# Row-sum reciprocals of a whole attention head spread by DMA, the head normalised in one operation, and one output copy per block

## The chip, the cores and the metric

The kernel runs on one core of one Trainium2 chip. The metric is the device time of one execution in microseconds (us), the median of several runs. A profile of one execution shows every instruction of the five engines: TensorE (PE, with its weight loads as PEld), VectorE (DVE), ScalarE (ACT), GpSimd (POOL) and SyncE (SP, which here only issues DMAs).

## The reference

One block of a metaformer on x of 8 images, 512 channels and 1024 positions, all in fp32: a channel layernorm, attention with 8 heads of 64 channels over the 1024 positions, a residual, a layernorm over channels, and a mixture of 16 experts that each choose their 128 best rows of every image.

```python
x = x + conv_ref(ln_c(x), Wq, bq, Wk, bk, Wv, bv, Wo, bo)
    # q, k, v = projections; scores = q k^T / 8 for each head
    # attn = softmax(scores); out = attn v; then the projection with Wo
t = to_tokens(x)
t = t + ffn_ref(ln_t(t), gate_weight, w1, b1, w2, b2)
    # logits = t gate; affinity = softmax(logits)
    # for each expert the top 128 rows: gelu(x w1 + b1) w2 + b2, times the gate, added back
x = from_tokens(t, x)
```

## The kernel before

`attention` runs first, over the 8 images one after the other; `experts` follows. Nothing of the two overlaps. Each engine has its own program, written out by hand in the order in which it issues; semaphores tie them together, so the order of the code is the schedule. To get fp32 precision from the fast matmul format every operand is split into a high part (written by ScalarE, `..._hi`) and a low part (the rest, `..._lo`), and products are the sum of high and low terms.

In an image, heads are taken in pairs. A pair has 16 units of 128 queries (8 for each head); the 64 units of an image are walked by a step number `s`. TensorE makes the scores of unit `s` (L834), VectorE their negated row maxima (L669), ScalarE the exponentials with their row sums `rsum` (L466). Two steps later TensorE turns the probabilities (L845) into the two-deep buffer `ring`, ScalarE writes the high part of `PT` (L475) and VectorE the low part (L727). Two units make a block `m` of 256 queries, 32 blocks in an image, 4 in a head. TensorE multiplies a block with `V` into the PSUM tile `O` (L877); half of the sum lies on the 64 partitions of the head and half on the other 64.

The normalisation of a block takes the rest of the engines. VectorE writes the reciprocals of its two columns of row sums (`rinv`, L735). GpSimd spreads each column over 128 columns (`rinv_bc`, L395, two instructions a block). TensorE turns both into the right half of `O` (`inverse_sums`, L889), so that the reciprocals lie along the columns. ScalarE copies three parts of 64 partitions out of PSUM (`copy_output`, L523 to L525: `Rs`, `oH`, `oL`). GpSimd adds the two halves (L410) and multiplies with the reciprocals (L413) into `oT`. From there `high_of_output` (ScalarE, L515) and `low_of_output` (GpSimd, L378) split the pieces of `oT` for the projection with Wo (`project_out`, L914). The pieces of the first three pairs are split while the last head still runs, at the steps of `EARLY_AT` and the blocks of `EARLY_BLOCK`.

The residual rows of x are loaded by SyncE late in the image, into `oT` and `spare`, as soon as the pieces that lay there are split. GpSimd adds the bias of the projection to them (`add_bo`, L384): tiles 0 to 3 beside the last two blocks, tiles 4 to 7 after the last piece. VectorE adds the projection to each tile (`tile_t`), takes its statistics, and between those normalises the next image's tiles `xt` (`normalise`, L630), in the order of the list `WRAP`. TensorE turns those tiles for the next image (L801) and projects V.

At the end of a pair TensorE projects q and k of the next pair (`project_pair`), and SyncE copies halves of k to the other partitions (`duplicate_k`) and loads the pair's weights (`load_pair`).

In `experts` the tiles are allocated one after the other; `b1s`, `idxc` and `gatec` have 32, 64 and 64 bytes to a partition and stand ahead of the larger tiles.

Of the kernel before, what the change touches and what calls it, by code (L numbers as in the profile page):

```python
# [16 lines left out]
F32 = mybir.dt.float32  # L17
F32R = mybir.dt.float32r
U32 = mybir.dt.uint32
# [58 lines left out]

def attention(nc, x, wT, b_row, b_col, gate, out, n2_dram, aff_dram, ident):
# [6 lines left out]
    wqk_dram, wv_dram = split_weights_dram(nc)  # L86
    with ExitStack() as ctx:
# [27 lines left out]
        def res(i):  # L115
# [5 lines left out]
        tmp = sb("tmp", [P, 3, 2, QC])  # L121
        Rs = tmp[:, 0, :, :]
        oL = tmp[:, 1, :, :]
        oH = tmp[:, 2, :, :]
        n2T = tmp[:, 0:2, :, :].rearrange("p a q c -> p a (q c)").rearrange(
            "p a (k t) -> p a k t", k=KC)
# [7 lines left out]
        ones = sb("ones", [P, P])  # L134
        rinv_bc = sb("rinv_bc", [P, 2, 2, P])
# [33 lines left out]
        res_in = [sem(f"res_in{i}") for i in range(2)]  # L169
# [27 lines left out]
        rbc_done = sem("rbc_done")  # L197
        pv_read = sem("pv_read")
        pv_done = sem("pv_done")
        o_copied = sem("o_copied")  # L200
        o_sum = sem("o_sum")
# [38 lines left out]
        def blocks_of_piece(j):  # L240

            if j < EARLY:
                return j // 2 * NT + QB + 2 * (j % 2) + 2
            return BLOCKS - QB + (j - EARLY) + 1
# [19 lines left out]
        def _(sp):  # L264
# [51 lines left out]
            def image(b, last):  # L316
# [11 lines left out]
                for k in range(2):  # L328
                    sp.wait_ge(os_lo, b * PIECES + 2 * k + 2)
                    sp.dma_start(dst[:, k, :, :], src[:, 2 * k:2 * k + 2, :]).then_inc(res_in[0], 16)  # L330
                sp.wait_ge(os_lo, b * PIECES + EARLY)
                sp.dma_start(dst[:, 2, :, :], src[:, 4:6, :]).then_inc(res_in[1], 16)
                sp.dma_start(spare[:, :, :], src[:, 6:8, :]).then_inc(res_in[1], 16)
# [26 lines left out]
        def _(pool):  # L360
# [8 lines left out]
            pool.wait_ge(ones_set, 1)  # L369
# [3 lines left out]
            def image(b, last):  # L373
                def low_of_output(j, blocks):
                    chunk, cols = piece(j)
                    pool.wait_ge(o_norm, b * BLOCKS + blocks)
                    pool.wait_ge(os_hi, b * PIECES + j + 1)
                    nc.gpsimd.tensor_tensor(oS[:, 1, chunk, cols], oT[:, chunk, cols],  # L378
                                            oS[:, 0, chunk, cols].bitcast(F32), ALU.subtract).then_inc(os_lo, 1)

                def add_bo(i):
                    if i % 4 == 0:
                        pool.wait_ge(res_in[i // 4], b * 32 + 32)
                    nc.gpsimd.tensor_tensor(res(i), res(i), bo_bc[:, :], ALU.add).then_inc(xbo, 1)  # L384

                for k in range(BLOCKS + 2):
                    if k < BLOCKS:
                        if k >= 3:
                            pool.wait_ge(o_norm, b * BLOCKS + k - 2)
                        pool.wait_ge(rinv_done, b * BLOCKS + k + 1)  # L390
                        if k >= 2:
                            pool.wait_ge(pv_done, b * BLOCKS + k - 1)
                        pool.sem_inc(pool_passed, 1)
# [4 lines left out]
                    if k >= 2:  # L398
                        m = k - 2
                        pair, odd, q = m // NT, m // QB % 2, m % QB  # L400
                        rows = slice(D * odd, D * odd + D)

                        if k < BLOCKS:
                            pool.wait_ge(rbc_done, b * BLOCKS + k + 1)
                        elif k == BLOCKS:
                            pool.wait_ge(xbo, b * NT + 4)
                        else:
                            pool.wait_ge(os_lo, b * PIECES + PIECES - 1)
                        pool.wait_ge(o_copied, b * BLOCKS + m + 1)
                        nc.gpsimd.tensor_tensor(oH[rows, m % 2, :], oH[rows, m % 2, :], oL[rows, m % 2, :],  # L410
                                                ALU.add).then_inc(o_sum, 1)
# [3 lines left out]
                        for j in range(EARLY):  # L415
                            if EARLY_BLOCK[j] == k:
                                low_of_output(j, m + 1)
                        if m >= BLOCKS - QB:
# [983 lines left out]
```

## Time and profile before

| | |
|---|---|
| time, median of 3 runs | 3360.12 us (3359.72 to 3362.19) |
| the profiled execution | 3358.84 us, its span in the trace 3357.0 us |
| TensorE busy | 3154.9 us, 94% of the span |
| VectorE busy | 2319.4 us, 69% |
| ScalarE busy | 2003.8 us, 60% |
| GpSimd busy | 1294.3 us, 39% |
| last image's attention ends | about 2485 us; the experts take the rest |

The busy share of an engine is an average over stages with different limits; ends of matmuls are modelled, so TensorE's pace is read from the distance between starts. In a timeline several like instructions that follow each other are merged into one row with their count; a bracket gives the idle time of the engine before the row and what ended it.

### The profile page before, as it was taken

Reading aid. Unit: us, or ns where it says so; the run is one execution under the profiler, and the core shown is the slowest. Engines: PE = TensorE matmul, PEld = TensorE weight load, DVE = VectorE, ACT = ScalarE, POOL = GpSimd, SP = SyncE. Lnnn points to the kernel's source line nnn. Section 1 sums busy time; section 2 is a strip of 40 time slices with the busy share of each in tenths; the row PEclk is TensorE's granted clock in tenths of the full one; section 3 lists DMA queues with packets and bytes.
Section 4 is the critical chain, followed back from the end, with each engine's and each line's share of the span. In section 5 each row is a group of like instructions: output and inputs, shape, how many; then the busy total and the mean of one; then the engine's idle time right before and its main releaser. Section 6 shows DMA issues by size and latency. Waiting matters only on the chain. (4 is left out here: it accounts for less than half of the span.)

```text
span 3357.0 us, 51875 instructions
## 1 busy us (share of the span) xinstructions
PE 3154.9 (94%) x18562; PEld 2696.9 (80%) x18562; DVE 2319.4 (69%) x3649; ACT 2003.8 (60%) x3833; POOL 1294.3 (39%) x1536
## 2 busy tenths in 40 slices
PE   6999999999999999999999999999944999999998
PEld 5888888788878888887888888888833888888886
DVE  5877687678768776875877677667766556555553
ACT  4876678478748856883887578478821333333332
POOL 1335234423523352343335234523432444444443
PEclk9999999999999999999999999999977999999999
DMA  6012111310220131112103211310132565655654
GB/s 219 26 51 101 52 51 39 113 52 26 82 96 26 51 109 51 44 51 101 52 27 101 77 41 40 111 39 26 39 114 61 135 133 126 142 136 120 149 136 59
DMA packets 108907, 268.82 MB, mean 80 GB/s; under 512 B 13456, under 2 KB 21648, under 8 KB 97936
## 3 DMA queue, kind: packets, MB, share of 16 engines
q1 hardware_dynamic: 80016, 198.80, 17.6%
q0 software_dynamic: 28672, 67.13, 11.2%
q8 instruction: 134, 2.20, 0.3%
q14 instruction: 85, 0.70, 0.1%
HBM read 158.40 MB, written 73.92 MB: 69 GB/s over the span
## 5 line engine op out<-in xcount | busy, mean ns | idle before, releaser
L727 DVE TENSOR_TENSOR PT<-ring,PT 128x512 fp32r<-128x512 f32 x1024 | 675.7, 685 | 230.8 <-ACT PT L475 221.8
L877 PE MATMUL O<-PT,V 128*128 128x256 f32 x4096 | 677.0, 290 | 0.0
L669 DVE TENSOR_REDUCE nmax<-S 128x1 f32<-128x1024 f32 x512 | 619.4, 1210 | 78.1 <-PE S L834 78.0
L395 POOL TENSOR_SCALAR rinv_bc<-ones,rinv 128x128 f32<-128x128 f32 x512 | 303.6, 605 | 934.3 <-DVE rinv L735 931.5
L845 PE MATMUL ring<-ident,prob 128*128 128x128 f32 x4096 | 617.2, 274 | 38.6 <-DVE qs L662 19.4
L475 ACT ACTIVATE PT<-ring 128x512 fp32r<-128x512 f32 x1024 | 582.1, 598 | 84.9 <-PE ring L845 70.5
L877 PEld LDWEIGHTS O<-PT,V 128*128 128x128 f32 x4096 | 577.7, 189 | 39.1
L466 ACT ACTIVATE prob<-S,nmax 128x1024 f32<-128x1024 f32 x512 | 571.7, 1117 | 56.3 <-DVE nmax L669 56.3
L834 PE MATMUL S<-kd,qs 128*128 128x512 f32 x2048 | 594.7, 414 | 3.4 <-DVE qs L662 2.3
L845 PEld LDWEIGHTS ring<-ident,prob 128*128 128x128 f32 x4096 | 460.3, 140 | 83.8 <-issue 70.4
L834 PEld LDWEIGHTS S<-kd,qs 128*128 128x128 f32 x2048 | 349.1, 189 | 55.5 <-ACT prob L466 2.8
L1356 PE MATMUL p<-ws,hT 128*128 128x512 f32 x1536 | 381.6, 400 | 0.0
L1319 PE MATMUL p<-xT,ws 128*128 128x512 f32 x1536 | 366.2, 397 | 1.5 <-DVE xT L1247 1.5
L1319 PEld LDWEIGHTS p<-xT,ws 128*128 128x128 f32 x1536 | 290.2, 189 | 72.3 <-issue 1.9
L1356 PEld LDWEIGHTS p<-ws,hT 128*128 128x128 f32 x1536 | 281.5, 188 | 61.9 <-DVE hT L1262 0.3
L1156 POOL DMA_INDIRECT out_dram<-y,idxc x128 | 203.2, 1588 | 291.7 <-ACT y L1224 264.3
L410 POOL TENSOR_TENSOR tmp<-tmp 64x256 f32<-64x256 f32 x256 | 189.1, 739 | 312.0 <-ACT tmp L525 292.5
L789 PE MATMUL ring<-nT,wqk 128*128 128x512 f32 x1152 | 267.3, 391 | 3.7 <-DVE PT L727 2.9
L789 PEld LDWEIGHTS ring<-nT,wqk 128*128 128x128 f32 x1152 | 214.4, 188 | 51.3 <-issue 7.9
L1212 ACT ACTIVATE hf<-p,b1s 128x512 f32<-128x512 f32 x128 | 88.2, 689 | 244.1 <-PE p L1319 244.1
L914 PE MATMUL S<-wo,nT 128*128 128x512 f32 x768 | 204.0, 418 | 0.0
L1199 ACT ACTIVATE xT<-xr 128x512 fp32r<-128x512 f32 x128 | 72.9, 598 | 207.9 <-PE xr L1329 207.9
(115 smaller groups left out, 3840.7 us busy)
## 6 DMA issues: line engine op xcount, KB each, us to landing
kd<-kd SPq DMA_DIRECT2D x128, 256.0 KB, 3.7
wraw<-w_dram SPq DMA_DIRECT2D x32, 1024.0 KB, 6.7
wqk<-wqk_split SPq DMA_DIRECT2D x24, 1024.0 KB, 4.8
xt<-x_dram SPq DMA_DIRECT2D x16, 1024.0 KB, 7.5
PT<-wv_split SPq DMA_DIRECT2D x7, 2048.0 KB, 8.2
oT<-x_dram SPq DMA_DIRECT2D x24, 512.0 KB, 3.6
out_dram<-oT SPq DMA_DIRECT2D x48, 256.0 KB, 8.3
n_rows<-oT SPq DMA_DIRECT2D x48, 256.0 KB, 2.3
```

The costliest lines, as they stand in the source:

```text
L395: last_bc = nc.gpsimd.tensor_scalar(rinv_bc[:, k % 2, j, :], ones[:, :], rinv[:, 2 * k + j:2 * k + j + 1], None, ALU.mult)
L466: nc.scalar.activation(prob[:, s % 2, :], S[:, s % 2, :], ACT.Exp, bias=nmax[:, s:s + 1], accum_out=rsum[:, s:s + 1]).then_inc(exp_done, 1)
L475: nc.scalar.activation(PT[:, 0, u // 2 % 2, 4 * c:4 * c + 4, u % 2 * P:u % 2 * P + P], ring[:, k % 2, :].rearrange("p (m q) -> p m q", m=4 ...
L669: nc.vector.tensor_reduce(nmax[:, s:s + 1], S[:, s % 2, :], AX.X, ALU.max, negate=True).then_inc(max_done, 1)
L727: nc.vector.tensor_tensor(PT[:, 1, here[0], here[1], here[2]], ring[:, k % 2, :].rearrange("p (m q) -> p m q", m=4), PT[:, 0, here[0], her ...
L789: last_mm = nc.tensor.matmul(dst, l, r, start=(n == 0), stop=(n == len(pairs) - 1))
L834: last_mm = nc.tensor.matmul(S[:, s % 2, 512 * m:512 * m + 512], qs[:, odd, i * P:(i + 1) * P], kd[:, odd, l, 512 * m:512 * m + 512], star ...
L845: last_t = nc.tensor.transpose(ring[:, k % 2, m * P:(m + 1) * P], prob[:, u % 2, (4 * c + m) * P:(4 * c + m + 1) * P], ident)
L877: last_mm = nc.tensor.matmul(O[:, m % 2, 0:QC], V[:, t, head // 2, 2 * (head % 2):2 * (head % 2) + 2, :].rearrange("p h d -> p (h d)"), PT ...
L914: last_mm = nc.tensor.matmul(S4[:, i % 4, :], oS[:, l, c, i * P:(i + 1) * P], wo[:, w, c, :], start=(c + n == 0), stop=(c == KC - 1 and n ...
L1319: last = nc.tensor.matmul(dst, l, r, start=(n == 0), stop=(n == len(pairs) - 1))
L1356: prod = nc.tensor.matmul(p2[:, j, :], hT[:, l, c, j * P:(j + 1) * P], ws[:, k, w, KC + c, :], start=(c + n == 0), stop=(c == KC - 1 and n ...
```

## The change

The reciprocals of heads 0 to 6 no longer go through GpSimd and TensorE. VectorE makes them once for a head (8 columns). SyncE writes them to a row of 1024 in DRAM and reads that row back to the 64 partitions of the head in the new tile `Rs` (`spread_inverse`, two DMAs and three waits in SyncE's program). GpSimd multiplies a whole head of `oT` with `Rs`, after its fourth block, in one instruction over 64 partitions and 1024 columns; it reads `Rs` with a step of 8 elements. The last head keeps the way through TensorE, block by block, but TensorE reads the column of `rinv` directly, with a step of 0, in place of the copy that GpSimd made.

`copy_output` is one copy of 128 partitions and 256 columns to `oHL`; for the last head a second one brings the reciprocals. GpSimd then moves the other half to the head's partitions (a copy, `oS2`) and adds both halves straight into `oT`. The wait of the copy for the block two before is now on this sum (`o_sum`) and no longer on the normalised block.

The residual loads and `add_bo` move: tiles 6 and 7 are loaded at the start of the image and added at block 5; tiles 0 to 5 are added at blocks 26 to 29 (`RES_TILES`), each ahead of that block's sum. In `experts`, the four small tiles are allocated last.

```diff
+RES_TILES = {5: [6, 7], 26: [0, 1], 27: [2], 28: [3, 4], 29: [5]}
+HEAD_UNITS = NT
+HEAD_BLOCKS = NT // 2
+NORMS = H - 1 + HEAD_BLOCKS
...
+    rinv_rows = nc.dram_tensor("rinv_rows", [H - 1, N], F32).ap()
...
-        tmp = sb("tmp", [P, 3, 2, QC])
...
+        Rs = sb("Rs", [P, N])
+        oHL = sb("oHL", [P, 2, QC])
+        oS2 = sb("oS2", [P, 2, QC])
...
-                for p in range(1, PAIRS):
-                    duplicate_k(b, p)
-                    if p < PAIRS - 1 or not last:
-                        sp.wait_ge(ring_filled, b * RING + ring_proj(p, 3) + 1)
-                        load_pair(p % (PAIRS - 1) + 1)
...
+                def spread_inverse(h):
+                    row, units = rinv_rows[h:h + 1, :], slice(HEAD_UNITS * h, HEAD_UNITS * h + HEAD_UNITS)
+                    odd = h % 2
+                    sp.wait_ge(rinv_done, b * NORMS + h + 1)
+                    sp.dma_start(row.rearrange("a (p u) -> p (a u)", p=P), rinv[:, units]).then_inc(rinv_out, 16)
+                    sp.wait_ge(rinv_out, b * (16 * (H - 1)) + 16 * h + 16)
+                    if h >= 2:
+                        sp.wait_ge(o_norm, b * NORMS + h - 1)
+                    sp.dma_start(Rs[D * odd:D * odd + D, :], row.broadcast_to([D, N])).then_inc(Rs_in[odd], 16)
+
+                load_residual(3)
+                for h in range(H - 1):
+                    if h % 2 == 1:
+                        p = h // 2 + 1
+                        duplicate_k(b, p)
+                        if p < PAIRS - 1 or not last:
+                            sp.wait_ge(ring_filled, b * RING + ring_proj(p, 3) + 1)
+                            load_pair(p % (PAIRS - 1) + 1)
+                    if h == H - 2:
+                        load_residual(0)
+                        load_residual(1)
+                    spread_inverse(h)
+                load_residual(2)
...
-                        for j in range(2):
-                            last_bc = nc.gpsimd.tensor_scalar(rinv_bc[:, k % 2, j, :], ones[:, :],
-                                                              rinv[:, 2 * k + j:2 * k + j + 1], None, ALU.mult)
-                        last_bc.then_inc(rbc_done, 1)
...
+                    for i in RES_TILES.get(m, []):
+                        add_bo(i)
...
+                    pool.wait_ge(o_copied, b * BLOCKS + m + 1)
+                    nc.gpsimd.tensor_copy(oS2[rows, m % 2, :], oHL[other, m % 2, :]).then_inc(o_shift, 1)
+                    pool.wait_ge(o_shift, b * BLOCKS + m + 1)
+                    nc.gpsimd.tensor_tensor(oT[rows, pair, cols], oHL[rows, m % 2, :], oS2[rows, m % 2, :],
+                                            ALU.add).then_inc(o_sum, 1)
+                    if head == H - 1:
                         pool.wait_ge(o_sum, b * BLOCKS + m + 1)
-                        nc.gpsimd.tensor_tensor(oT[rows, pair, q * QC:(q + 1) * QC], oH[rows, m % 2, :],
-                                                Rs[rows, m % 2, :], ALU.mult).then_inc(o_norm, 1)
...
+                    elif q == HEAD_BLOCKS - 1:
+                        pool.wait_ge(o_sum, b * BLOCKS + m + 1)
+                        pool.wait_ge(Rs_in[odd], b * (16 * (PAIRS - odd)) + 16 * pair + 16)
+                        whole = oT[rows, pair, :].rearrange("d (u p) -> d u p", p=P)
+                        nc.gpsimd.tensor_tensor(whole, whole, Rs[rows, :].rearrange("d (p u) -> d u p", p=P),
+                                                ALU.mult).then_inc(o_norm, 1)
...
-                for i in range(4, NT):
-                    add_bo(i)
...
                     act.wait_ge(pv_done, b * BLOCKS + m + 1)
+                    if m >= BLOCKS - HEAD_BLOCKS:
+                        cols = slice(m % HEAD_BLOCKS * QC, m % HEAD_BLOCKS * QC + QC)
+                        nc.scalar.activation(Rs[D:2 * D, cols], O[D:2 * D, m % 2, QC:2 * QC], ACT.Copy)
                     if m >= 2:
-                        act.wait_ge(o_norm, b * BLOCKS + m - 1)
-                    nc.scalar.activation(Rs[rows, m % 2, :], O[rows, m % 2, QC:2 * QC], ACT.Copy)
-                    nc.scalar.activation(oH[rows, m % 2, :], O[rows, m % 2, 0:QC], ACT.Copy)
-                    nc.scalar.activation(oL[rows, m % 2, :], O[other, m % 2, 0:QC], ACT.Copy).then_inc(o_copied, 1)
+                        act.wait_ge(o_sum, b * BLOCKS + m - 1)
+                    nc.scalar.activation(oHL[:, m % 2, :], O[:, m % 2, 0:QC], ACT.Copy).then_inc(o_copied, 1)
...
+                    group = HEAD_UNITS if u < UNITS - HEAD_UNITS else 2
+                    if u % group == group - 1:
+                        units = slice(u + 1 - group, u + 1)
                         dve.wait_ge(exp_done, b * UNITS + u + 1)
-                        nc.vector.reciprocal(rinv[:, u - 1:u + 1], rsum[:, u - 1:u + 1]).then_inc(rinv_done, 1)
+                        nc.vector.reciprocal(rinv[:, units], rsum[:, units]).then_inc(rinv_done, 1)
...
-                    pe.wait_ge(rbc_done, b * BLOCKS + m + 1)
+                    if m < BLOCKS - HEAD_BLOCKS:
+                        return
+                    pe.wait_ge(rinv_done, b * NORMS + H - 1 + m - (BLOCKS - HEAD_BLOCKS) + 1)
                     for j in range(2):
                         last_t = nc.tensor.transpose(O[:, m % 2, QC + j * P:QC + (j + 1) * P],
-                                                     rinv_bc[:, m % 2, j, :], ident)
+                                                     rinv[:, 2 * m + j:2 * m + j + 1].broadcast_to([P, P]), ident)
                     last_t.then_inc(pv_done, 1)
...
-        b1s = sb("b1s", [P, 2, KC])
-        b2s = sb("b2s", [P, 2, C])
-        idxc = sb("idxc", [P, 2, B], U32)
-        gatec = sb("gatec", [P, 2, B])
         xg = sb("xg", [P, 2, G, C])
...
+        b2s = sb("b2s", [P, 2, C])
+        b1s = sb("b1s", [P, 2, KC])
+        idxc = sb("idxc", [P, 2, B], U32)
+        gatec = sb("gatec", [P, 2, B])
```

## Rows read from the trace of the kernel before

**Rows 1.** The page: the span.

```profile
span 3357.0 us, 51875 instructions
```

**Rows 2.** Windows: length, busy time of PE, PEld, DVE, ACT, POOL, PEclk, DMA.

```profile
134.00:168.20 34.20, 34.20 (x252) 31.83 (x251) 29.40 (x42) 32.08 (x66) 15.69 (x24) 1.00 0.01 1
269.00:288.00 19.00, 18.09 (x132) 16.53 (x131) 15.14 (x22) 17.94 (x39) 13.56 (x18) 1.00 0.21 65
310.00:330.00 20.00, 16.31 (x69) 13.10 (x68) 18.55 (x34) 3.59 (x8) 8.87 (x9) 0.83 0.51 188
2602.08:2651.12 49.04, 48.59 (x227) 39.25 (x225) 28.44 (x49) 15.20 (x24) 21.45 (x18) 1.00 0.60 135
```

**Rows 3.** Timeline of TensorE, one block of a middle head.

```profile
702.15 1.17 PE L834 MATMUL S<-kd,qs 128*128 128x512 f32 x4
...
704.90 1.17 PE L834 MATMUL S<-kd,qs 128*128 128x512 f32 x4
...
707.27 0.60 PE L845 MATMUL ring<-ident,prob 128*128 128x128 f32 x4
707.71 0.38 PE L889 MATMUL O<-ident,rinv_bc 128*128 128x128 f32 x2
707.84 0.48 PE L834 MATMUL S<-kd,qs 128*128 128x512 f32 x1
```

**Rows 4.** Timeline of TensorE, after a pair change and beside the early pieces.

```profile
133.63 0.38 PE L889 MATMUL O<-ident,rinv_bc 128*128 128x128 f32 x2
...
139.47 0.38 PE L889 MATMUL O<-ident,rinv_bc 128*128 128x128 f32 x2
...
269.34 0.38 PE L889 MATMUL O<-ident,rinv_bc 128*128 128x128 f32 x2
...
277.62 0.63 PE L845 MATMUL ring<-ident,prob 128*128 128x128 f32 x4 [0.29 <-DVE PT L727]
...
287.95 0.38 PE L889 MATMUL O<-ident,rinv_bc 128*128 128x128 f32 x2
```

**Rows 5.** Timeline between images 0 and 1.

```profile
312.48 6.62 DVE L630 TENSOR_SCALAR xt<-xt,mv,rstd 128x512 f32<-128x512 f32 x6
...
313.13 3.02 PE L914 MATMUL S<-wo,nT 128*128 128x512 f32 x12
...
314.53 2.88 POOL L384 TENSOR_TENSOR oT<-oT,bo_bc 128x512 f32<-128x512 f32 x2
317.37 2.84 POOL L384 TENSOR_TENSOR spare<-spare,bo_bc 128x512 f32<-128x512 f32 x2
...
319.84 1.09 PE L801 MATMUL ring<-ident,xt 128*128 128x128 f32 x4 [3.69 <-DVE nT L636]
...
320.58 5.25 PE L914 MATMUL S<-wo,nT 128*128 128x512 f32 x12
```

**Rows 6.** Groups of instructions by line and shape: count, busy us, mean ns.

```profile
L395 POOL TENSOR_SCALAR rinv_bc<-ones,rinv 128x128 f32<-128x128 f32 x512 | 303.6, 605 | 934.3 <-DVE rinv L735 931.5 <-issue 2.8
...
L410 POOL TENSOR_TENSOR tmp<-tmp 64x256 f32<-64x256 f32 x256 | 189.1, 739 | 312.0 <-ACT tmp L525 292.5 <-POOL rinv_bc L395 0.6
...
L525 ACT ACTIVATE tmp<-O 64x256 f32<-64x256 f32 x256 | 97.0, 379 | 3.0
...
L384 POOL TENSOR_TENSOR oT<-oT,bo_bc 128x512 f32<-128x512 f32 x48 | 63.4, 1342 | 0.0
...
L630 DVE TENSOR_SCALAR oT<-oT,mv,rstd 128x512 f32<-128x512 f32 x48 | 25.7, 537 | 0.0
```

**Rows 7.** DMA issues: count, KB each, median us to landing.

```profile
affinities<-oT SPq DMA_DIRECT2D x8, 64.0 KB, 1.9
...
bv_bc<-b_row_dram SPq DMA_DIRECT2D x1, 256.0 KB, 9.7
```

**Rows 8.** Timeline: head 1's last reciprocals, and its last block's copy.

```profile
132.44 0.15 DVE L735 RECIPROCAL rinv<-rsum 128x2 f32<-128x2 f32 x1
...
145.13 0.38 ACT L525 ACTIVATE tmp<-O 64x256 f32<-64x256 f32 x1
```

More of the change, by code:

```diff
@@ L168, in attention @@
         x_in = [sem(f"x_in{i}") for i in range(2)]
-        res_in = [sem(f"res_in{i}") for i in range(2)]
+        res_in = [sem(f"res_in{i}") for i in range(4)]
+        rinv_out = sem("rinv_out")
+        Rs_in = [sem(f"Rs_in{i}") for i in range(2)]
         wv_in = sem("wv_in")
@@ L381, in add_bo @@
                 def add_bo(i):
-                    if i % 4 == 0:
-                        pool.wait_ge(res_in[i // 4], b * 32 + 32)
+                    pool.wait_ge(res_in[i // 2], b * 16 + 16)
                     nc.gpsimd.tensor_tensor(res(i), res(i), bo_bc[:, :], ALU.add).then_inc(xbo, 1)
[L386 to L393, printed above, removed]
-                        for j in range(2):
-                            last_bc = nc.gpsimd.tensor_scalar(rinv_bc[:, k % 2, j, :], ones[:, :],
-                                                              rinv[:, 2 * k + j:2 * k + j + 1], None, ALU.mult)
-                        last_bc.then_inc(rbc_done, 1)
[L398 to L411, printed above, removed]
-                        pool.wait_ge(o_sum, b * BLOCKS + m + 1)
-                        nc.gpsimd.tensor_tensor(oT[rows, pair, q * QC:(q + 1) * QC], oH[rows, m % 2, :],
-                                                Rs[rows, m % 2, :], ALU.mult).then_inc(o_norm, 1)
[L415 to L418, printed above, removed]
-                            low_of_output(EARLY + m - (BLOCKS - QB), m + 1)
-                        if BLOCKS - 2 <= k < BLOCKS:
-                            for i in range(2):
-                                add_bo(2 * (k - BLOCKS + 2) + i)
@@ L423, in image, with tiles_added, pieces_split, norms_made @@
-                for i in range(4, NT):
-                    add_bo(i)
+                def tiles_added(m):
+                    return sum(len(v) for k, v in RES_TILES.items() if k <= m)
+                def pieces_split(m):
+                    return sum(k - 2 < m for k in EARLY_BLOCK) + max(0, m - (BLOCKS - QB))
+                def norms_made(m):
+                    return m // HEAD_BLOCKS if m <= BLOCKS - HEAD_BLOCKS else H - 1 + m - (BLOCKS - HEAD_BLOCKS)
+                for m in range(BLOCKS):
+                    head, q = m // HEAD_BLOCKS, m % HEAD_BLOCKS
+                    pair, odd = head // 2, head % 2
+                    rows, other = slice(D * odd, D * odd + D), slice(D * (1 - odd), D * (1 - odd) + D)
+                    cols = slice(q * QC, (q + 1) * QC)
+                    if m:
+                        pool.wait_ge(o_sum, b * BLOCKS + m)
+                        pool.wait_ge(o_norm, b * NORMS + norms_made(m))
+                    for i in RES_TILES.get(m, []):
+                        add_bo(i)
+                    if m in RES_TILES:
+                        pool.wait_ge(xbo, b * NT + tiles_added(m))
+                    if pieces_split(m):
+                        pool.wait_ge(os_lo, b * PIECES + pieces_split(m))
+                    pool.wait_ge(o_copied, b * BLOCKS + m + 1)
[4 more added lines that the diff above has]
+                    if head == H - 1:
+                        pool.wait_ge(o_sum, b * BLOCKS + m + 1)
+                        nc.gpsimd.tensor_tensor(oT[rows, pair, cols], oT[rows, pair, cols], Rs[rows, cols],
+                                                ALU.mult).then_inc(o_norm, 1)
[4 more added lines that the diff above has]
+                        nc.gpsimd.tensor_tensor(whole, whole, Rs[rows, :].rearrange("d (p u) -> d u p", p=P),
+                                                ALU.mult).then_inc(o_norm, 1)
+                    for j in range(EARLY):
+                        if EARLY_BLOCK[j] == m + 2:
+                            pool.wait_ge(o_sum, b * BLOCKS + m + 1)
+                            pool.wait_ge(o_norm, b * NORMS + norms_made(m + 1))
+                            low_of_output(j)
+                    if m >= BLOCKS - QB:
+                        low_of_output(EARLY + m - (BLOCKS - QB))
```

46 lines of the change are left out of this document (17 added, 29 removed).

## Prediction

> **What bounds the kernel now.** I read the page first, then the windows of four stretches, then the timeline of one block. The span is 3357.0 us [rows 1]. In the middle of a head TensorE is busy all 34.20 us of a stretch of 34.20 us, at the full clock [rows 2]: it is the bound there, and ScalarE (32.08 us) follows close behind. That busy figure alone would not settle it, because ends of matmuls are modelled; the timeline of a block does. Its two halves start with the scores at 702.15 and 704.90 and the next block starts at 707.84 [rows 3], with no bracket of idle time between them. So the halves take 2.75 and 2.94 us and the block 5.69 us, and the half that holds the two turns of the reciprocals (L889) is the longer one by 0.19 us.
>
> Two other kinds of stretch are slower than that pace. Beside the early pieces three blocks take from 269.34 to 287.95, 6.20 us each, and a row of TensorE there waits for VectorE's low part [rows 4]; ScalarE is busy 17.94 of 19.00 us in that window [rows 2], so it is the late engine. After a pair change a block takes 139.47 - 133.63 = 5.84 us [rows 4]; three such blocks follow each of three pair changes. And between two images VectorE is busy 18.55 of 20.00 us while TensorE's granted clock falls to 0.83 of full speed [rows 2]. There six normalises of the next image take 6.62 us, while GpSimd runs the four bias additions, and TensorE waits 3.69 us for what follows them [rows 5]. In the experts TensorE is busy 48.59 of 49.04 us [rows 2].
>
> **The change part by part.**
>
> The turns of the reciprocals (L889) go from 28 of 32 blocks. Their price on TensorE's path: the difference of the halves says 0.19 us; four like turns take 707.71 - 707.27 = 0.44 us, so two take 0.22 us [rows 3]. The bounds are 0.13 us (start of L889 to the next start) and 0.38 us (its own busy time). I take 0.21 us. At the three pair changes the projections stand around the turns and I have no row that prices them there, so I count 25 blocks: 25 x 8 images x 0.21 = 42 us (the three would add 5 us). The bounds give 26 to 76 us, but the upper one counts overlap twice.
>
> The copies out of PSUM: two of three go for those blocks, 0.38 us each [rows 6]; a copy of 128 partitions has the same 256 columns, and I price it like one of 64. ScalarE loses some 0.7 us a block. In the 6.20 us blocks that brings ScalarE under TensorE's pace, so they fall to it: 3 x (6.20 - 5.69) = 1.5 us an image; the nine blocks after pair changes give 9 x 0.15 = 1.4 us. Together 2.9 x 8 = 23 us, between 0 (the wait moves to VectorE) and 23. Elsewhere the relief is off the path and counts nothing, but it gives room: VectorE and ScalarE both have more spare time beside the new 5.48 us than beside the old 5.69. At a pair change the relief could give up to the wait that I did not price; I leave it as the margin on the fast side, 10 us in all.
>
> The bias additions move. Tiles 6 and 7 go to block 5 and tiles 4 and 5 to blocks 28 and 29, ahead of the last pieces. GpSimd's work from 314.53 to 320.21 [rows 5] is gone from there. The same normalise takes 0.537 us on the `oT` tiles [rows 6], so six of them take 3.2 us and not 6.62: VectorE comes 3.4 us earlier to the low part for which TensorE waits. TensorE then doesn't idle 3.69 us, and its next 12 products, which took 5.25 us at the lower clock, take the 3.02 us of the 12 before them [rows 5], 2.2 us less. The sum is 5.6 us; as VectorE is nearly full in this stretch, part of the second term hides behind it. I take 4.5 us for each of seven boundaries, 31 us, between 0 and 39. The rows show two-fold normalises while both engines work. The Trainium skill, "SBUF — State Buffer", section "Who interferes with whom", states that a two-port VectorE instruction (such as a tensor_scalar within SBUF) and a GpSimd instruction exclude each other for a whole instruction. By that rule the move gives the 3.4 us only as long as no other GpSimd work takes the place of the additions; it is what the second rival below rests on.
>
> GpSimd's own sum: a block loses two spreads of 0.605 us and the multiply (like L410, 0.739 us), and gains a shift of 64x256, between 0 and 0.739 us [rows 6]. A head gains one multiply of four times the columns, at most 4 x 0.739 = 3.0 us if its stepped read costs nothing more. For four blocks that is at most 4 x 1.48 + 3.0 = 8.9 us of some 22 us: it hides under TensorE's pace. Without the spreads no wait of TensorE on GpSimd is left in these heads.
>
> The round trip of the reciprocals: 4 KB out and 256 KB back. No row shows either. The nearest are 1.9 us (64 KB out to DRAM) and 9.7 us (256 KB broadcast at the start, among large loads) [rows 7]; two legs lie between 3.8 and 19.4 us. I take 3 us a leg, nearer the first, as the queue is quiet here. The time that hides it: a head's last reciprocals come at 132.44 and its last copy begins at 145.13, 12.7 us later [rows 8], and GpSimd needs the row only after that block's sum. Behind that wait in GpSimd's queue stands the next block's sum; ScalarE needs it only two blocks on, so another 16.4 us (three blocks) less GpSimd's own 6 us are covered. The two legs at 19.4 us still fit into 12.7 + 10. In SyncE's queue `duplicate_k` stands ahead of each odd head's round trip and the even heads end half a pair before the next one, so k is not late; `load_residual(2)` waits behind head 6's round trip and is needed at block 28.
>
> The rest: larger reciprocals cost nothing visible (0.15 us [rows 8] once for a head). The new order of the experts' tiles changes no instruction; TensorE has 0.45 us of idle time for each expert [rows 2], so at most 16 x 0.45 = 7 us; I take 0.
>
> Sum: 42 + 23 + 31 = 96 us.
>
> **The rivals.**
>
> First, TensorE's pace does not follow: what was L889 becomes a wait for VectorE's low part in the two-deep `ring`. For it: in rows 4 such waits of 0.3 us appear when ScalarE is late. Against it: the other half of the block already runs at 2.75 us with the same ring work. Then 23 + 31 = 54 us remain: 3306 us.
>
> Second, the gain between images fails: GpSimd now has three operations for each of blocks 28 to 31, and ahead of them two additions of 1.34 us; if these run into the normalises they are held up as before. For it: each of the last blocks has a shift more. Against it: GpSimd's last piece ended at 314.53 before [rows 5]; two spreads (1.2 us) and the two additions between the last blocks (2.7 us) are gone from ahead of it, and up to three shifts (2.2 us) come in, so I estimate its end at 312.8 us at the latest, where the normalises begin at 312.48. Then 42 + 23 = 65 us remain: 3295 us.
>
> Third, slower: the round trip comes too late, GpSimd stands at the head's multiply, ScalarE's copy stands on `o_sum`, TensorE on `o_copied`. It decides from 12.7 + 10 = 23 us after the reciprocals. At 26 us each of 56 heads loses 3 us, 168 us against 96 gained: 3432 us. Rows bound both legs at 19.4 us, so little is left for it, unless the multiply itself is long. The Trainium skill, "GPSIMD Engine Reference", section "Performance pitfalls for Q7 kernels", states that reads with a step over 8 bytes cost about half as much again; by it the 3.0 us would be an estimated 4.5 us, which alone decides nothing. No row here has such a read.
>
> Fourth, no change: the path would have to lie elsewhere. The 34.20 of 34.20 us speaks against it.
>
> **How the numbers follow.** The profiled execution took 3358.84 us, so the forecast for it is 3263 us; the median of the runs is 1.3 us above it, and I predict 3264 us. Chances: forecast 0.70, pace 0.12, boundary 0.12, slower 0.04, no change 0.02. The fast end adds the pair changes (10 us), the rest of the boundary term (8 us) and the experts' bound (7 us): 3239. The slow end takes in both rivals: 3308. A measurement tells about 0.2% (7 us) from no change. Faster holds 0.94, the same 0.02, slower 0.04.
>
> **What would show it.** The same block should start its scores 5.48 us apart, both halves near 2.75 us. The blocks beside the early pieces should take about 5.5 us. The normalises between images should take 0.54 us each, no GpSimd row of L384's kind beside them, and the granted clock of that stretch should stay near 1.00. TensorE's waits should show no new row for `o_copied` (ScalarE's copy), and GpSimd none of length for the DMA into `Rs`. Wrong would be a bracket of VectorE's low part in each block, GpSimd rows beside the normalises, or idle time of GpSimd ahead of the head's multiply that reaches ScalarE.

## The result, and the profile after

The changed kernel takes 3239.05 us (median of four runs, 3235.94 to 3241.66) beside 3359.92 us of the kernel before on the same chip: a ratio of 0.964, 95% interval 0.9624 to 0.9657. It gained 121 us where 96 were forecast, so the time stands 25 us below the predicted 3264 us, at the fast edge of the range. The profiled execution took 3238.71 us.

The page of the changed kernel, its span and its engines:

```profile
span 3236.9 us, 49715 instructions
...
PE 3057.5 (94%) x18114; PEld 2630.2 (81%) x18114; DVE 2279.6 (70%) x3481; ACT 1848.2 (57%) x3353; POOL 1089.6 (34%) x1112
```

TensorE's timeline in the middle of a head (to be laid beside [rows 3]):

```profile
683.34 1.17 PE L863 MATMUL S<-kd,qs 128*128 128x512 f32 x4
...
686.07 1.17 PE L863 MATMUL S<-kd,qs 128*128 128x512 f32 x4
687.08 0.62 PE L906 MATMUL O<-PT,V 128*128 128x256 f32 x4
687.54 0.60 PE L874 MATMUL ring<-ident,prob 128*128 128x128 f32 x4
...
688.80 1.17 PE L863 MATMUL S<-kd,qs 128*128 128x512 f32 x4
```

Both halves of the block now take 2.73 us (686.07 - 683.34 and 688.80 - 686.07), the block 5.46 us and not 5.69. The blocks beside the early pieces, which took 6.20 us, take the same now, and those after pair changes nearly so. The boundary between images 0 and 1 (beside [rows 5]):

```profile
304.20 2.82 DVE L657 TENSOR_SCALAR xt<-xt,mv,rstd 128x512 f32<-128x512 f32 x6
...
304.78 3.02 PE L945 MATMUL S<-wo,nT 128*128 128x512 f32 x12
307.74 0.42 PEld L830 LDWEIGHTS ring<-ident,xt 128*128 128x128 f32 x4 [0.36 <-issue]
...
308.15 3.00 PE L945 MATMUL S<-wo,nT 128*128 128x512 f32 x12
```

The six normalises take 2.82 us for 6.62, no GpSimd row stands beside them, TensorE's wait of 3.69 us is gone, and the next 12 products take 3.00 us for 5.25. Before, TensorE's granted clock fell to the lower of its two levels (1.2 GHz, the upper is 2.4) during that wait, and the mean of the stretch was 0.83. The windows of the changed kernel (columns as in [rows 2]) show the granted clock of that stretch at 1.00:

```profile
133.00:167.00 34.00, 33.79 (x247) 31.33 (x246) 30.25 (x39) 29.73 (x57) 11.04 (x15) 1.00 0.06 17
262.00:282.00 20.00, 19.83 (x148) 18.47 (x146) 17.25 (x25) 18.04 (x37) 16.09 (x17) 1.00 0.29 94
300.00:320.00 20.00, 19.53 (x98) 15.72 (x97) 17.58 (x43) 3.54 (x7) 2.17 (x3) 1.00 0.65 244
```

The round trip in head 1 (beside [rows 8]), and its prices among the groups by shape and the DMA issues:

```profile
131.49 0.19 DVE L764 RECIPROCAL rinv<-rsum 128x8 f32<-128x8 f32 x1
131.71 0.33 SPq L339 DMA_DIRECT2D rinv_rows<-rinv  x1
...
133.12 0.48 SPq L343 DMA_DIRECT2D Rs<-rinv_rows  x1
...
144.46 3.09 POOL L444 TENSOR_TENSOR oT<-oT,Rs 64x1024 f32<-64x1024 f32 x1
```

```profile
L434 POOL TENSOR_TENSOR oT<-oHL,oS 64x256 f32<-64x256 f32 x256 | 188.5, 737 | 20.5
L444 POOL TENSOR_TENSOR oT<-oT,Rs 64x1024 f32<-64x1024 f32 x56 | 169.9, 3034 | 4.4
L432 POOL COPY oS<-oHL 64x256 f32<-64x256 f32 x256 | 100.5, 393 | 1304.1 <-ACT oHL L552 1299.0 <-POOL nT L401 3.9
```

```profile
Rs<-rinv_rows SPq DMA_DIRECT2D x56, 256.0 KB, 3.4
rinv_rows<-rinv SPq DMA_DIRECT2D x56, 4.0 KB, 1.4
```

The legs take 1.4 and 3.4 us, so the reciprocals lie in `Rs` 5.0 us after they were made (133.12 + 3.4 - 131.49), 8 us ahead of the multiply.

Where the 120.1 us between the two spans lie, by the starts of TensorE's scores, products with Wo and expert products in the two traces, summed over the images:

| stretch | before | after | gain | forecast |
|---|---|---|---|---|
| unit 3 to unit 63, eight images | 1696.3 | 1625.0 | 71.3 | 65 |
| first to last product with Wo, seven boundaries | 243.2 | 202.8 | 40.4 | 31 |
| around these: last score to first product, last product to next score | 357.3 | 362.9 | -5.6 | 0 |
| last image: last product with Wo to first expert product | 109.7 | 106.4 | 3.3 | 0 |
| first expert product to the end | 792.2 | 781.4 | 10.8 | 0 |
| the rest (start, first three units, last image's products) | 158.2 | 158.5 | -0.3 | 0 |

The stretch between the last image's products and the first expert product varies from 104.7 to 109.7 us over all kernels of this study, in no order that follows their edits, so its 3.3 us are not explained below. The forecast had the experts at 0, because the instructions there are the same. Why the stretches around the products lose 5.6 us was not looked into.

### The profile page after: what moved, and what is told of

Its sections match the earlier page's. It is cut to its first block and busy times, and to the rows that moved or that the text cites. A ratio compares the mean times of both kernels' runs of the same rounds, so it can differ in the third digit from the quotient of the medians.

```text
span 3236.9 us, 49715 instructions
## 1 busy us (share of the span) xinstructions
PE 3057.5 (94%) x18114; PEld 2630.2 (81%) x18114; DVE 2279.6 (70%) x3481; ACT 1848.2 (57%) x3353; POOL 1089.6 (34%) x1112
## 5 line engine op out<-in xcount | busy, mean ns | idle before, releaser
L432 POOL COPY oS<-oHL 64x256 f32<-64x256 f32 x256 | 100.5, 393 | 1304.1 <-ACT oHL L552 1299.0
L1387 PE MATMUL p<-ws,hT 128*128 128x512 f32 x1536 | 375.5, 397 | 0.4 <-DVE hT L1293 0.4
L1350 PE MATMUL p<-xT,ws 128*128 128x512 f32 x1536 | 356.1, 391 | 1.5 <-DVE xT L1278 1.5
L434 POOL TENSOR_TENSOR oT<-oHL,oS 64x256 f32<-64x256 f32 x256 | 188.5, 737 | 20.5
L945 PE MATMUL S<-wo,nT 128*128 128x512 f32 x768 | 191.3, 398 | 0.0
```

The costliest lines, as they stand in the source:

```text
L945: last_mm = nc.tensor.matmul(S4[:, i % 4, :], oS[:, l, c, i * P:(i + 1) * P], wo[:, w, c, :], start=(c + n == 0), stop=(c == KC - 1 and n ...
L1350: last = nc.tensor.matmul(dst, l, r, start=(n == 0), stop=(n == len(pairs) - 1))
L1387: prod = nc.tensor.matmul(p2[:, j, :], hT[:, l, c, j * P:(j + 1) * P], ws[:, k, w, KC + c, :], start=(c + n == 0), stop=(c == KC - 1 and n ...
```

## The experiments

### The order of the experts' tiles

The tiles that the change moves behind the others have 32, 4096, 64 and 64 bytes to a partition, 32 over a multiple of 128. Before, they put xT and hT 32 bytes past a multiple of 128; after, both stand on one. `e1` is the kernel before with the four small tiles moved behind `base_f`, `e2` the changed kernel with them back ahead of `xg`:

```diff
-        b1s = sb("b1s", [P, 2, KC])
-        b2s = sb("b2s", [P, 2, C])
-        idxc = sb("idxc", [P, 2, B], U32)
-        gatec = sb("gatec", [P, 2, B])
         xg = sb("xg", [P, 2, G, C])
...
         base_f = sb("base_f", [P, B, E])
+        b2s = sb("b2s", [P, 2, C])
+        b1s = sb("b1s", [P, 2, KC])
+        idxc = sb("idxc", [P, 2, B], U32)
+        gatec = sb("gatec", [P, 2, B])
```

> The kernel before, with nothing changed but the order in which the experts' tiles are allocated (the small ones last, so that xT and hT stand 32 bytes further towards an aligned place). Theory, the address of an operand sets TensorE's pace: the 512-column matmuls of the experts start 0.227 us apart and not 0.234 and 0.232, the experts lose about 10 us, the attention nothing, and the whole is about 3350 us. Rival, the order does nothing and the experts' gain came from elsewhere (the attention's end, the DMAs' times): 3360 us and the old distances.

> The changed kernel with the old order of the experts' tiles. Theory, the address: distances of 0.234 and 0.232 us return in the experts, which end about 10 us later, near 3249 us; the attention keeps its whole gain (it ends near 2371 us). Rival: no change, 3239 us, and 0.227 us stays.

`e1` took 3346.28 us, ratio 0.9963 (0.9949 to 0.9976): 12 us gained by four moved lines. `e2` took 3252.16 us, 13 us more than the changed kernel. Forty-eight expert products in a row, in the timelines of the kernel before, then of `e1`:

```profile
3004.90 11.40 PE L1319 MATMUL p<-xT,ws 128*128 128x512 f32 x48
3016.13 1.04 PE L1329 MATMUL xr<-ident,xg 128*128 128x128 f32 x8
```

```profile
2995.95 11.05 PE L1319 MATMUL p<-xT,ws 128*128 128x512 f32 x48
3006.83 1.03 PE L1329 MATMUL xr<-ident,xg 128*128 128x128 f32 x8
```

From the first start to the start of the next row that is 11.23 and 10.88 us for 48, 0.234 and 0.227 us for one. The attention's rows do not move. The theory of the address holds, the rival falls. Next, which address counts? The experts' first products move xT, the second hold hT as weights. `e3` moves xT by 32 bytes with 8 unused elements ahead and 8 behind, `e4` hT (16 ahead of xT, 8 on either side of hT):

```diff
+        pad0 = sb("pad0", [P, 8])
         xT = sb("xT", [P, 2, 2, KC, COLS], F32R)
+        pad1 = sb("pad1", [P, 8])
         hf = sb("hf", [P, 2, COLS])
```

> The changed kernel with xT alone moved by 32 bytes (8 unused elements ahead and behind; hT and all else stay at places that are multiples of 64 bytes). Theory, it is the moving operand's own address: the products that move xT (L1352 here) start 0.234 us apart, those that hold hT stay at 0.227 us; some 4 to 6 us more than the changed kernel. Rival, any tile's place shifts all (a matter of banks or of the gathers beside them): both distances move, or neither.

> The changed kernel with hT alone moved by 32 bytes past a multiple of 64 (xT moved by 64 bytes, to a multiple of 64 still). hT is the held operand, loaded as weights, of the second products, while what they move stays where it was. Theory, a held operand's address matters as well: the second products start 0.232 us apart, the first stay at 0.227 us; some 3 to 5 us more than the changed kernel. Rival, only the moving operand's address matters: both stay at 0.227 us and the time is that of the changed kernel, 3239 us.

`e3` took 3251.38 us and `e4` 3244.98 us, but in `e3` the second products slowed too (their group's busy time is 382.1 us, 375.5 in the changed kernel), against the theory. My unit was wrong: with 64 bytes of padding hT had come to 64 past a multiple of 128. The next four move one tile at a time and put the others back on multiples of 128 (`e9`: 8 elements ahead of xT, 24 behind; `e10`: 16 and 16 around hT; `e11`: 16 behind hT; `e12`: 96 ahead of the first tile).

> The changed kernel with xT alone 32 bytes past a multiple of 128 (8 unused elements ahead of it, 24 behind, so that hT and all tiles after it stand at multiples of 128 as in the changed kernel). In the run that moved xT by 32 bytes with 8 elements on either side, hT came to 64 past a multiple of 128 and the second products slowed too. Theory, each operand's own place modulo 128 bytes counts: here the first products start 0.234 us apart and the second stay at 0.227; the experts lose 7 to 9 us. Rival, the place of the other tiles or of both together counts: the second slow as well, or neither.

> The changed kernel with hT alone 64 bytes past a multiple of 128 (16 unused elements ahead, 16 behind). Theory, a held operand, loaded as weights, wants a multiple of 128: the second products start 0.232 to 0.234 us apart, the first stay at 0.227; some 5 us more. Rival, a multiple of 64 is enough for it, and the second products slowed earlier for the place of hf or y: 0.227 us and no more time.

> The changed kernel with all the tiles behind hT (y0, y, work and the small ones, read and written by VectorE, ScalarE, GpSimd and the DMAs, not by TensorE) 64 bytes past a multiple of 128, xT and hT in their places. Theory, the place of TensorE's operands counts: both distances stay at 0.227 us and the time is that of the changed kernel. Rival, other engines' accesses to misplaced tiles take TensorE's reads: distances of 0.23 us or more, 5 to 10 us more.

> The changed kernel with all the experts' large tiles at multiples of 512 bytes (96 unused elements ahead of the first; in the changed kernel they stand 128 past one). Theory, a multiple of 128 is enough: 0.227 us and no change of time. Rival, the rule goes on and a multiple of 512 is better still: distances under 0.227 us (0.213 us would be a column a cycle at 2.4 GHz), up to 20 us less, which would beat both kernels.

They took 3245.80, 3241.66, 3240.37 and 3237.84 us (ratio of the last 0.9645, 0.9629 to 0.9661: not to be told from the changed kernel). The groups of the two kinds of products, in the changed kernel, `e9` and `e10`:

```profile
L1387 PE MATMUL p<-ws,hT 128*128 128x512 f32 x1536 | 375.5, 397 | 0.4 <-DVE hT L1293 0.4
...
L1350 PE MATMUL p<-xT,ws 128*128 128x512 f32 x1536 | 356.1, 391 | 1.5 <-DVE xT L1278 1.5
```

```profile
L1389 PE MATMUL p<-ws,hT 128*128 128x512 f32 x1536 | 380.6, 400 | 0.2 <-DVE hT L1295 0.2
...
L1352 PE MATMUL p<-xT,ws 128*128 128x512 f32 x1536 | 363.6, 395 | 1.6 <-DVE xT L1280 1.6
```

```profile
L1389 PE MATMUL p<-ws,hT 128*128 128x512 f32 x1536 | 381.8, 401 | 0.1
...
L1352 PE MATMUL p<-xT,ws 128*128 128x512 f32 x1536 | 354.0, 389 | 1.5 <-DVE xT L1280 1.5
```

In `e10` only the products that hold hT lose (6 us of busy time), at 64 past a multiple of 128; most of it disappears in shorter waits, and the run is 2.6 us over the changed kernel, no more than its runs scatter. In `e9` those that move xT lose 7.5 us; but the second products lose 5 us as well, with hT in its place. That part of the theory falls, and why is open. Writes into the misplaced xT do not show as the reason: in the trace of `e9` the second products beside such writes start 0.232 us apart, the others 0.233. What differs is that they never settle: in the changed kernel the first nine distances behind each row of turns average 0.230 us and the later ones 0.227; in `e9` both average 0.232 to 0.233. `e11` shows that the tiles behind hT, which TensorE does not read, may stand 64 bytes past, `e12` that 512 is no better than 128.

### The turns and the copies

`e5` adds two dead turns (work that nobody reads) to each block of heads 0 to 6, `e6` two dead copies ahead of the block's own copy, `e13` both:

```diff
                     if m < BLOCKS - HEAD_BLOCKS:
+                        for j in range(2):
+                            nc.tensor.transpose(O[:, m % 2, QC + j * P:QC + (j + 1) * P], ident, ident)
                         return
...
+                    else:
+                        for j in range(2):
+                            nc.scalar.activation(dead[D * j:D * j + D, :], O[D * j:D * j + D, m % 2, 0:QC], ACT.Copy)
```

> The changed kernel with dead work added: in heads 0 to 6 TensorE turns the identity twice into the unused right half of O after each block's products, as many 128x128 turns as the change took away, with no wait and no reader. Theory, the turns were on the path by their own price: each half with them takes about 0.2 us more, the blocks go from 5.46 to about 5.67 us, 28 x 8 x 0.21 = 47 us, so about 3286 us. Rival, the turns lay beside other work and the pace came from the rest (fewer copies, no wait for GpSimd): about 3239 us with no change of the halves.

> The changed kernel with dead work added: in heads 0 to 6 ScalarE makes two more copies of 64x256 out of O after each block's copy, into a tile that nobody reads, so that it has as many copies as before. Theory, ScalarE is late only after pair changes and beside the early pieces: some 23 us more (3262 us), and the other blocks stay at 5.46 us. Rivals: ScalarE sets the pace of all blocks once TensorE is faster (2 x 0.38 us x 224 blocks = 170 us at most); or it is nowhere late, 3239 us.

> The changed kernel with both pieces of dead work at once: two turns of the identity by TensorE and two copies of 64x256 by ScalarE for each block of heads 0 to 6. Alone the turns cost some 47 us and the copies some 55. Theory, both hold the same half of the block, by two different ways (TensorE's own work and a wait of its ring for a late ScalarE), so that they cost little more together than one alone: 55 to 72 us over the changed kernel, 3295 to 3311 us, with halves of 2.75 and 2.94 us as before the change. Rival, they add up: 102 us, 3341 us, and blocks of 5.9 us.

`e5` took 3283.05 us, 44 more than the changed kernel, as expected: one half of each block takes 2.98 us and the other stays near 2.75. The longer half is the one that ends with the turns (here written `O<-ident`), as in [rows 3]:

```profile
685.00 1.17 PE L863 MATMUL S<-kd,qs 128*128 128x512 f32 x4
...
687.84 0.38 PE L918 MATMUL O<-ident 128*128 128x128 f32 x2
687.98 1.17 PE L863 MATMUL S<-kd,qs 128*128 128x512 f32 x4
...
690.72 1.17 PE L863 MATMUL S<-kd,qs 128*128 128x512 f32 x4
```

`e6` took 3293.42 us, 54 more, where 23 were expected, and not only the blocks beside the early pieces slow down: nearly all have halves of some 2.75 and 2.92 to 2.95 us. `e13` took 3298.57 us, 60 more and not the sum of 98. So the copies alone cost a block about as much as the turns alone, but in its other half, not in the same one as was expected for `e13`. How they do it is seen in the timeline of `e6`:

```profile
686.74 1.17 PE L867 MATMUL S<-kd,qs 128*128 128x512 f32 x4
...
689.46 1.17 PE L867 MATMUL S<-kd,qs 128*128 128x512 f32 x4
690.47 0.62 PE L910 MATMUL O<-PT,V 128*128 128x256 f32 x4
691.11 0.63 PE L878 MATMUL ring<-ident,prob 128*128 128x128 f32 x4
...
692.41 1.18 PE L867 MATMUL S<-kd,qs 128*128 128x512 f32 x4
```

```profile
688.60 0.76 ACT L553 ACTIVATE dead<-O 64x256 f32<-64x256 f32 x2
689.37 0.38 ACT L556 ACTIVATE oHL<-O 128x256 f32<-128x256 f32 x1
689.65 1.08 ACT L504 ACTIVATE PT<-ring 128x512 fp32r<-128x512 f32 x2
```

The half at whose end the copies run (in `e5` it ends with the turns) takes 2.72 us (689.46 - 686.74); the next one takes 2.95 (692.41 - 689.46). ScalarE reaches the high part of `PT` only behind its three copies, at 689.65, 0.19 us after the scores; VectorE's low part follows, frees the ring, and TensorE's turns start at 691.11, 0.64 us after the products at 690.47. In the changed kernel above the same two rows lie 0.46 us apart (687.08 and 687.54). TensorE loses 0.18 us a block and no bracket tells of it, since the modelled end of the products covers the gap: only the starts do. In `e13` the turns stand ahead of the same scores:

```profile
690.54 1.08 ACT L504 ACTIVATE PT<-ring 128x512 fp32r<-128x512 f32 x2
690.60 1.17 PE L867 MATMUL S<-kd,qs 128*128 128x512 f32 x4
691.60 0.64 PE L910 MATMUL O<-PT,V 128*128 128x256 f32 x4
692.08 0.60 PE L878 MATMUL ring<-ident,prob 128*128 128x128 f32 x4
```

They hold TensorE back just long enough for ScalarE: its high part begins 0.06 us before the scores, the turns follow the products after 0.48 us again, and that half takes 2.75 us. From the starts of the scores, the units of eight images take 47.4 us more than the changed kernel with the turns alone, 55.9 with the copies alone and 63.1 with both.

### The bias additions

`e7` puts the additions of tiles 4 to 7 back behind GpSimd's last piece; `e8` is the kernel before with only the loads and additions moved (of its edit, the lines added to GpSimd's program):

```diff
-RES_TILES = {5: [6, 7], 26: [0, 1], 27: [2], 28: [3, 4], 29: [5]}
+RES_TILES = {26: [0, 1], 27: [2], 28: [3]}
...
+                for i in range(4, NT):
+                    add_bo(i)
```

```diff
...
+                        tiles = {7: [6, 7], 28: [0, 1], 29: [2], 30: [3, 4], 31: [5]}.get(k, [])
+                        if tiles:
+                            pool.wait_ge(o_norm, b * BLOCKS + k - 1)
+                        for i in tiles:
+                            add_bo(i)
...
```

> The changed kernel with the bias additions of tiles 4 to 7 back behind GpSimd's last piece (their loads stay where the change put them). Theory, GpSimd's additions beside VectorE's normalises cost the boundary: six normalises take about 6 us again and not 2.82, each of seven boundaries some 5.5 us more, 38 us, so about 3277 us. Rival, the additions hide and the boundary gained by something else: 3239 us.

> The kernel before with only the residual loads and bias additions moved: tiles 6 and 7 loaded at the image's start and added beside block 5, tiles 0 to 5 beside blocks 26 to 29, with the waits that this order needs in GpSimd's queue. Theory, the boundary's gain belongs to this part alone: seven boundaries each 4.5 to 5.5 us shorter, 31 to 38 us, so 3322 to 3328 us, unless GpSimd, which still spreads reciprocals here, is late beside the last blocks: then part of it is lost and its pieces run into the normalises. Rival, the move is worth nothing without the rest: 3359 us or more.

`e8` took 3319.19 us, ratio 0.9886 (0.987 to 0.9903), a gain of 37 us: its seven boundaries go from 243.2 to 205.4 us, its blocks do not change. The part works by itself. `e7` took 3257.22 us, only 18 more than the changed kernel, half of what was expected. Its timeline at a boundary:

```profile
595.99 2.54 POOL L406 TENSOR_TENSOR oT<-oT,bo_bc 128x512 f32<-128x512 f32 x2
...
598.47 4.85 DVE L659 TENSOR_SCALAR xt<-xt,mv,rstd 128x512 f32<-128x512 f32 x6
598.49 2.72 POOL L406 TENSOR_TENSOR spare<-spare,bo_bc 128x512 f32<-128x512 f32 x2
604.07 0.63 PE L832 MATMUL ring<-ident,xt 128*128 128x128 f32 x4 [2.67 <-DVE nT L665]
```

Two of the four additions are over when the normalises begin; in [rows 5] all four had to end behind their start. I put it down to GpSimd's program, where the spreads and the additions of tiles 0 to 2 no longer lie between its last pieces; this was not tried by itself. So the normalises take 4.85 us, between 2.82 and 6.62, and TensorE waits 2.67 us.

### A longer round trip

`e14` reads the row of reciprocals four times in place of once, `e15` eight times:

```diff
+                    for t in range(3):
+                        sp.dma_start(Rs[D * odd:D * odd + D, :], row.broadcast_to([D, N])).then_inc(trip_in, 16)
+                        sp.wait_ge(trip_in, b * (16 * (H - 1) * 3) + 16 * (h * 3 + t) + 16)
                     sp.dma_start(Rs[D * odd:D * odd + D, :], row.broadcast_to([D, N])).then_inc(Rs_in[odd], 16)
```

> The changed kernel with the read of the reciprocals' row into Rs made four times, one after the other, and only the last one signalled: the round trip is three reads of about 3.4 us longer, some 15 us in place of 4.8. Theory, 23 us of cover behind a head's last reciprocals: no change, 3239 us. Rival, the cover ends at the 12.7 us to GpSimd's multiply, and all beyond is paid: some 2 us x 56 = 112 us more at most.

> The same with eight reads: seven of 3.4 us more, a round trip of about 29 us, 6 us past the 23 us of cover. Theory: GpSimd stands at the multiply until ScalarE's copy and with it TensorE wait for its sum: up to 6 us for each of 56 heads, 336 us at most, and less where the wait falls into a pair change of 17.6 us; odd heads' trips also delay the weights of the next pair. Rival, the cover is longer than 29 us: no change, 3239 us.

`e14` took 3267.74 us, 29 more than the changed kernel, and `e15` 3714.03 us, ratio 1.1061 (1.1042 to 1.1079). In `e14` the units take 1625.9 us for 1625.0: in the heads the longer trip is hidden, though GpSimd now waits for it. All of the loss is between the images (230.7 us for 202.8, and 28.6 for 26.9 in the last), behind head 6. GpSimd's timeline of `e14` there:

```profile
559.96 3.10 POOL L448 TENSOR_TENSOR oT<-oT,Rs 64x1024 f32<-64x1024 f32 x1 [2.94 <-DMA Rs<-rinv_rows]
...
586.18 3.10 POOL L448 TENSOR_TENSOR oT<-oT,Rs 64x1024 f32<-64x1024 f32 x1 [7.18 <-DMA Rs<-rinv_rows]
```

Head 6's trip starts late: SyncE first issues the residual loads 0 and 1, which wait for the early pieces. And behind its multiply there are no three blocks of cover, but additions and the last head's pieces, which the projection needs. In the changed kernel's timeline:

```profile
559.02 0.19 DVE L764 RECIPROCAL rinv<-rsum 128x8 f32<-128x8 f32 x1
...
562.84 0.49 SPq L343 DMA_DIRECT2D Rs<-rinv_rows  x1
...
572.09 3.00 POOL L444 TENSOR_TENSOR oT<-oT,Rs 64x1024 f32<-64x1024 f32 x1
```

The read is issued 3.8 us behind the reciprocals (1.6 in head 1), and with 3.4 us for it this head has 5.8 us to spare (572.09 - 562.84 - 3.4), not the 18 that 23 less 5.0 would leave. In `e15` the units too take 327.6 us more, on average 5.9 us for each of 56 heads, and the boundaries another 142. That this is near my 6 is chance, for the loss has more than one cause. In heads 1, 3 and 5 TensorE does wait at the end of the chain through GpSimd's multiply and ScalarE (its copy, or its first early pieces); the units lose 216 us there, some 7 to 13 us a head. The other 111 us lie at the three pair changes, where k comes late, as its copies stand behind the trip in SyncE's queue:

```profile
831.36 3.75 PE L867 MATMUL S<-kd,qs 128*128 128x512 f32 x8 [4.13 <-issue]
```

The last copy of k was issued there at 825.89, and such a copy takes 4.4 us in this run. The granted clock of the whole span falls as well, to 0.93 from 0.98 in the changed kernel.

## Why the prediction was right or wrong

**The step that failed** is the last of the sum: "The new order of the experts' tiles changes no instruction; TensorE has 0.45 us of idle time for each expert [rows 2], so at most 16 x 0.45 = 7 us; I take 0." The premise is true and the bound isn't one: idle time bounds what a shorter wait can give, and here the busy time shrank. The same first products start 0.227 us apart and not 0.234 now that their operands stand on multiples of 128 bytes, and the group of the second went from 381.6 to 375.5 us. This was worth 10.8 us in the traces, 12 and 13 us in `e1` and `e2`, out of the 25 us by which the forecast was off.

**Two terms were too small.** The boundaries gave 40.4 - 5.6 = 34.8 us for 31: the discount from 5.6 to 4.5 us a boundary, for the part of the clock's recovery that might hide behind VectorE, was mostly not due (40.4 / 7 = 5.8 us between the products themselves). The blocks gave 71 us for 65: the 25 halves with turns 0.23 us each and not 0.21 (45.9 for 42), the blocks beside the early pieces 12.2 for 12 and those after pair changes 10.5 for 11. The pair changes, 10 us on the fast side, gave nothing to speak of: 17.62 us from score to score for 17.69.

**The blocks' sum was near by place, but not by cause.** I gave the turns 42 us and the copies 23, and held that elsewhere the copies' relief "is off the path and counts nothing". `e5` bears out the turns (44 us when put back alone); `e6` refutes the rest: put back alone the copies cost 54 us, through a wait in the half behind them. While the turns were there they covered that wait, because the 0.2 us that TensorE spent on them gave ScalarE the time. By these sums dropping the turns with the copies kept would have won some 7 us of 42 (63.1 less 55.9), and dropping the copies with the turns kept some 16 of 23 (63.1 less 47.4, of which 12 beside the early pieces). That is nearly my first rival (a wait for VectorE's low part takes the place of L889), and it failed to come only because both went. My argument against it, that the other half already ran at 2.75 us, was no argument: it is this other half that `e6` slows, and it ran at 2.75 us because the turns stood ahead of it. The three blocks beside the early pieces are the copies' as forecast: halves of 3.44 us in `e6`, 2.98 in `e5`. The nine after pair changes aren't: in `e13`, with turns and copies, most of their halves are 2.75 and 2.98 us, where the kernel before had up to 2.89 and 2.98. What else made them long (GpSimd's spreads, or the copy's wait on the normalised block) was not tried.

**Right:** no new wait for GpSimd in the heads, and the shift (0.393 us). The head's multiply came at 3.0 us as priced, though by luck. An unstepped subtraction of GpSimd takes 739 ns for 256 columns and 1291 ns for 512 (L401), less than twice as long, so a straight line gives an estimated 2.4 us for 1024 columns, not four times the 64x256 sum; the 3034 ns with one operand stepped by 32 bytes are about a quarter more than that. The Trainium skill, "GPSIMD Engine Reference", section "Performance pitfalls for Q7 kernels", adds about half for reads with a step over 8 bytes. These runs show less, as far as that estimate goes; no run has an unstepped multiply of this size. The second rival rested on the Trainium skill, "SBUF — State Buffer", section "Who interferes with whom". The trace agrees with the mechanism (six normalises take 4.85 us in `e7` and 2.82 us with no additions beside them), but GpSimd's last piece ended at 302.83 us, 1.4 us before the normalises began.

**Right by luck:** the third rival. It put the deciding point at 23 us for every head. For heads 0 to 5 the runs only bracket it (about 15 us cost nothing, about 29 us cost time in heads 1, 3 and 5), and the rival left out that a long trip in SyncE's queue makes k late as well. Head 6 has its own point: with trips of some 15 us, 29 us over the eight images were lost already, so the prediction's sentence that two legs at 19.4 us still fit does not hold there. What carried the forecast is that the legs were short: 1.4 us, less than any row shown, and 3.4.

## What to carry to other kernels

Idle time bounds only what a shorter wait can give; an edit that moves addresses can change the pace of every instruction that reads them, so compare the distance between starts in stages that the change leaves alone, and try matmul operands on multiples of 128 bytes. Before an edit is priced from one engine's row, ask which engine that work was giving time to, in the next half of the block too: two costs that cover each other are won in full only together, and put back one at a time they add to more than the gain. For a hidden transfer look for the one instance with the least cover (here the last before a stage ends), not the typical one.

## What the runs showed of the hardware that was not expected

In the experts the products that move xT start 0.227 us apart when xT stands on a multiple of 128 bytes, and 0.233 to 0.234 us when it stands 32 past one. For the operand held as weights 64 past is enough to lose (381.8 us for 375.5 of the group); for the moved one 64 past cost little (357.2 us for 356.1 in `e4`). With xT 32 past, the products that do not read it lost 5 us also; that is open. In every one of these rows TensorE counted as busy nearly throughout.
